# ScalarE takes the rows' mean and variance, VectorE a PSUM copy: a fused embed, attention and FFN kernel

## The reference

```python
h = concatenate([patch_rows, text_rows], axis=1)          # 64 x 228 x 192
h = h + attention(layernorm(h))
h = h + ffn(layernorm(h))

def bitlinear(x, w, g):
    xn = rmsnorm(x, g)                    # x * rsqrt(mean(x*x) + 1e-6) * g
    xq = act_quant(xn)                    # per row: round(xn * 127 / max|xn|), and back
    return einsum('bsd,fd->bsf', xq, ternary(w))
def ffn(x):
    return bitlinear(gelu(bitlinear(x, w1, g1)), w2, g2)   # 192 -> 768 -> 192
```

## Time and profile before

| what | value |
|---|---|
| median of 3 runs | 1753.07 us (1752.8 to 1753.71) |
| the profiled execution | 1751.31 us |
| its span, first to last instruction | 1749.6 us |
| mean granted TensorE clock | 0.913 |
| PE busy | 1473.4 us (84%) |
| DVE busy | 1461.2 us (84%) |
| ACT busy | 1232.4 us (70%) |
| POOL busy | 1099.7 us (63%) |

### The profile page before, as it was taken

How to read it: one execution, slowest core, us unless ns; L and a number is a source line. 1 busy time by engine, 2 the same in 40 slices (tenths; PEclk the granted TensorE clock), 3 DMA queues, 4 the chain that set the end, 5 groups by cost and what they waited for, 6 DMA issues and landing times.

```text
span 1749.6 us, 53766 instructions
## 1 busy us (share of the span) xinstructions
PE 1473.4 (84%) x18602; PEld 1203.6 (69%) x18602; DVE 1461.2 (84%) x3227; ACT 1232.4 (70%) x1862; POOL 1099.7 (63%) x1369
## 2 busy tenths in 40 slices
PE   5799999999999999999999999985556565656565
PEld 2688888888888888888888888874454454544454
DVE  5588888888888888888888888874899999999996
ACT  0476666667676776767667676653688888888887
POOL 5456565656666665666665656542777777777775
PEclk9899999999999999999999999996677877777876
DMA  8533334343434343434343333320000000000000
GB/s 209 78 60 68 61 63 65 61 67 60 68 60 68 59 69 55 72 53 74 53 72 56 70 58 68 60 56 18 9 24 20 24 20 24 20 24 20 24 20 29
DMA packets 104194, 93.57 MB, mean 53 GB/s; under 512 B 22737, under 2 KB 94466, under 8 KB 104162
## 3 DMA queue, kind: packets, MB, share of 16 engines
q1 hardware_dynamic: 103394, 91.58, 27.7%
q0 software_dynamic: 768, 1.57, 0.4%
HBM read 74.12 MB, written 11.91 MB: 49 GB/s over the span
## 4 chain that ended last, share of the span: by engine, by line
PE 66%; DVE 20%; issue 7%; ACT 3%; POOL 1%; DVEq 1%; DMA 0%; SPq 0%; ACTq 0%; POOLq 0%
PE ps L1039 19%; PE ps L1096 9%; PE ps L1182 8%; DVE nmax L677 6%; PE ps L1173 5%; PE ps L1129 5%; DVE ff_st L813 4%; PE ps L1280 3%; PE ps L1161 3%; PE ps L1155 3%; PE ps L1261 3%; PE ps L1134 2%; PE ps L1077 2%; PE ps L1110 2%; DVE xpix L806 1%
## 5 line engine op out<-in xcount | busy, mean ns | idle before, releaser
L1039 PE MATMUL ps<-w_eff,pix 124*112 124x193 f32 (+1 forms) x2048 | 406.8, 337 | 10.4 <-DMA pix<-side 8.4
L677 DVE TENSOR_REDUCE nmax<-ps 116x12 bf16<-116x1344 f32 (+2 forms) x192 | 302.9, 1577 | 87.1 <-PE ps L1134 87.1
L493 POOL TENSOR_TENSOR pix<-probs,g_b 112x192 f32<-112x192 f32 (+1 forms) x512 | 298.0, 612 | 103.5 <-ACT probs L994 94.2
L882 ACT ACTIVATE probs<-ps,isw 116x688 f32<-116x688 f32 x384 | 298.9, 831 | 84.6 <-PE ps L1161 83.2
L1039 PEld LDWEIGHTS ps<-w_eff,pix 124*112 124x112 f32 (+1 forms) x2048 | 308.3, 167 | 37.2 <-issue 22.0
L420 POOL TENSOR_TENSOR xsq<-xsq 124x784 f32<-124x784 f32 (+1 forms) x128 | 184.4, 1441 | 216.1 <-ACT xsq L875 211.1
L440 POOL TENSOR_SCALAR_AFFINE_SELECT probs<-probs 116x464 f32<-116x464 f32 x384 | 274.1, 726 | 68.9 <-ACT probs L882 60.4
L1250 PE MATMUL ps<-ident_h,xpix 112*96 112x112 f16 (+1 forms) x256 | 34.9, 281 | 193.8 <-DVE xpix L830 187.9
L864 ACT ACTIVATE pix<-xpix 54x896 f32<-54x896 f32 (+1 forms) x128 | 196.6, 1538 | 1.2 <-DMA xpix<-in_x 0.4
L1096 PE MATMUL ps<-xnT,wq_pad 97*128 97x228 f32 (+1 forms) x768 | 166.5, 366 | 0.0
L1250 PEld LDWEIGHTS ps<-ident_h,xpix 112*96 112x96 f16 (+1 forms) x256 | 23.8, 167 | 205.0 <-issue 103.3
(11 more groups left out here) (134 smaller groups left out, 3175.1 us busy)
## 6 DMA issues: line engine op xcount, KB each, us to landing
xpix<-in_x SPq DMA_DIRECT2D x192, 196.0 KB
rden<-den_rows SPq DMA_DIRECT2D x256, 85.5 KB, 2.2
out<-xpix SPq DMA_DIRECT2D x64, 87.0 KB
out<-xpix SPq DMA_DIRECT2D x64, 84.0 KB
xpix<-in_x SPq DMA_DIRECT2D x128, 34.1 KB
h_all<-shift_w SPq DMA_DIRECT2D x5, 768.0 KB, 4.4
pix<-side SPq DMA_DIRECT2D x64, 36.8 KB
pix<-side SPq DMA_DIRECT2D x64, 36.6 KB
```

Source lines behind the costliest of these rows:

```text
L493: last = nc.gpsimd.tensor_tensor(v2[0:P, b, tile, cols], gel[0:P, b, tile, cols], g2_b[0:P, cols], ALU.mult)
L677: V.tensor_reduce(dst, src, AX_X, ALU.max, negate=True).then_inc(s_mx, 1)
L882: A(probs[0:TB, g, 2 * e:2 * e + 2, :], ps[0:TB, 4 + 2 * e:6 + 2 * e, 0:SK], ACT.Exp, scale=isw[0:TB, 7:8]).then_inc(s_p, 1)
L1039: last = MM(ps_tok[tile][0:P, :], pix[0:HI, par, o, lo:lo + P], w_eff[0:HI, o, :], start=(o == 0), stop=(o == OFFS - 1))
```

## The change

The mean and the variance of the FFN's input rows move from VectorE in the FFN stage to ScalarE in the attention stage. `row_means(n - 1)` sums a row with a Copy of scale -1/192 into `mean2`, `row_squares(n - 1)` sums (h - mean)^2 into `row_ssq`, each with the accumulator of the ACTIVATE, two tiles each. GpSimd's `row_roots(n - 2)` turns that into the roots and keeps them for all images in `roots`. In the FFN stage VectorE no longer runs bn_stats, bn_aggr and the first mean square; it copies the turned rows (`copy_rows_turned`, which ScalarE did), and the product scales are a separate instruction (`weigh_steps`, with a semaphore `f_step`). Its order is now v1, y, copy_rows_turned, weigh_steps, max of v1, mean square of gelu, max of v2, the chain, q1. ScalarE's order is quantise, squares, copy of q2T, gelu; the squares of image i are now in step i. TensorE's order is turn_first(m), turn_second(j), ffn_first(m), ffn_second(j). GpSimd's pow in the FFN stage has two columns.

```diff
+            def row_roots(m):
+                pool.wait_ge(s_rsq, 2 * m + 2)
+                after(pool, s_rms, m)
+                apart(pool)
+                nc.gpsimd.tensor_scalar(ln_st[:, 32:34], row_ssq[:, :], (1.0 + EPS_RMS) / DIM, EPS_LN * EPS_RMS,
+                                        ALU.mult, ALU.add).then_inc(s_var2, 1)
+                pool.wait_ge(s_var2, m + 1)
+                nc.gpsimd.tensor_tensor(roots[:, bass.ds(m * 4, 2)], ln_st[:, 32:34], expo[:, 0:2],
+                                        ALU.pow).then_inc(s_rms, 1)
...
                 if newer:
                     patch_roots(n + 2)
+                if prev:
+                    row_roots(n - 2)
                 if old:
                     clear_later(n, 0)
...
+            def copy_rows_turned(m):
+                dve.wait_ge(f_t1, m + 1)
+                after(dve, f_m1, 2 * m)
+                src = bank16(0, 4 * TB, F16).rearrange("p (t c k) -> p t c k", t=2, c=2)
+                for tile, P in enumerate((TA, TB)):
+                    ins = V.tensor_scalar(q1T[0:HALF, tile, :, 0:P], src[0:HALF, tile, :, 0:P], -MAGIC16, None, ALU.add)
+                ins.then_inc(f_t1s, 1)
+
+            def weigh_steps(i, b):
+                after(dve, f_g, 2 * i)
+                V.tensor_tensor(ff_st[:, b, 40:44], ff_st[:, b, 28:32], w_step[:, :], ALU.mult).then_inc(f_step, 1)
...
-                if new:
-                    apart(dve)
-                    for tile, P in enumerate((TA, TB)):
-                        ins = V.bn_stats(st[0:P, 6 * tile:6 * tile + 6], h_all[0:P, hcols(m, tile)])
-                    flink(ins)
-                    apart(dve)
-                    for tile, P in enumerate((TA, TB)):
-                        ins = V.bn_aggr(st[0:P, 12 + 2 * tile:14 + 2 * tile], st[0:P, 6 * tile:6 * tile + 6])
-                    flink(ins)
...
+                if turned:
+                    copy_rows_turned(m - 1)
+                if steps_:
+                    weigh_steps(i - 1, 1 - b)
...
                 if mid:
-                    dve.wait_ge(f_v2, 2 * j + 2)
+                    dve.wait_ge(f_ssq, 2 * j + 2)
+                    V.tensor_scalar(st[:, 18:20], gel_sum[:, 1 - b, :], 1.0 / HIDDEN, EPS_RMS, ALU.mult,
+                                    ALU.add).then_inc(f_var, 1)
...
-                    V.tensor_tensor(st[:, 40:44], st[:, 28:32], w_step[:, :], ALU.mult)
...
+            def row_means(n):
+                act.wait_ge(s_h2, n + 1)
+                after(act, s_rsq, 2 * n)
+                apart(act)
+                for tile, P in enumerate((TA, TB)):
+                    A(spare[0:P, tile, :], h_all[0:P, hcols(n, tile)], ACT.Copy, scale=-1.0 / DIM,
+                      accum_out=mean2[0:P, bass.ds(n * 2 + tile, 1)]).then_inc(s_mean2, 1)
+
+            def row_squares(n):
+                after(act, s_var2, n)
+                for tile, P in enumerate((TA, TB)):
+                    act.wait_ge(s_mean2, 2 * n + tile + 1)
+                    apart(act)
+                    A(spare[0:P, tile, :], h_all[0:P, hcols(n, tile)], ACT.Square,
+                      bias=mean2[0:P, bass.ds(n * 2 + tile, 1)],
+                      accum_out=row_ssq[0:P, tile:tile + 1]).then_inc(s_rsq, 1)
...
                 if newest:
                     edge_squares(n + 3, par)
+                if prev:
+                    row_means(n - 1)
                 if old:
                     copy_attended(n, 2, 3)
...
                     regroup_even(n + 4, 1 - par, coming, 0)
+                if prev:
+                    row_squares(n - 1)
                 if new:
                     copy_maxima(n + 1)
...
-            def ffn_step(i, new=True, mid=True, last_=True):
+            def ffn_step(i, new=True, mid=True):
                 if new:
                     turn_first(i + 1)
-                if last_:
-                    ffn_second(i - 2)
+                if mid:
+                    turn_second(i - 1)
                 if new:
                     ffn_first(i + 1)
                 if mid:
-                    turn_second(i - 1)
+                    ffn_second(i - 1)
```

More of the change, by code:

```diff
@@ L527, in _ @@
             step(V.memset(ff_st[:, :, :], 1.0))
+            step(V.memset(mean2[:, :], 1.0))
+            step(V.memset(row_ssq[:, :], 1.0))
+            step(V.memset(roots[:, :], 1.0))
             step(V.memset(gel_sum[:, :, :], 1.0))
@@ L727, in step_images @@
                     maxima(n + 1, 0)
+                if new:
                     maxima(n + 1, 1)
@@ L768, in ffn_step @@
+            def weigh_steps(i, b):
+                after(dve, f_g, 2 * i)
+                V.tensor_tensor(ff_st[:, b, 40:44], ff_st[:, b, 28:32], w_step[:, :], ALU.mult).then_inc(f_step, 1)
+            def ffn_step(i, b, new=True, mid=True, last_=True, turned=True, steps_=True, skipped=0):
                 m, j, st = i + 1, i - 1, ff_st[:, b, :]
                 flinks[:] = [0, (i + 1) * F_LINKS - skipped]
-                if new or mid:
-                    after(dve, f_g, 2 * i)
-                    after(dve, f_q2, i - 2)
@@ L834, in _ @@
             dve.wait_ge(s_h2, IMAGES - 1)
-            ffn_step(-1, 1, mid=False, last_=False)
+            dve.wait_ge(s_rms, 1)
+            dve.wait_ge(s_mean2, 2)
+            ffn_step(-1, 1, mid=False, last_=False, turned=False, steps_=False)
+            copy_rows_turned(0)
+            weigh_steps(-1, 1)
             step_images(IMAGES, 1, None, old=False, new=False, newer=False)
             dve.wait_ge(s_h2, IMAGES)
-            ffn_step(0, 0, mid=False, last_=False)
+            dve.wait_ge(s_rms, IMAGES)
+            dve.wait_ge(s_mean2, 2 * IMAGES)
+            ffn_step(0, 0, mid=False, last_=False, turned=False, steps_=False)
             ffn_step(1, 1, last_=False)
@@ L947, in _ @@
             act.wait_ge(s_vset, V_SETUP)
-            step_images(-2, 1, 1, 2, old=False, new=False)
-            step_images(-1, 0, 0, 2, old=False)
+            step_images(-2, 1, 1, 2, prev=False, old=False, new=False)
+            step_images(-1, 0, 0, 2, prev=False, old=False)
             act.wait_ge(s_text[1], 64)
-            step_images(0, 1, 1, 3)
+            step_images(0, 1, 1, 3, prev=False)
             step_images(1, 0, 0, 3)
@@ L976, in quantise, with ffn_step @@
                     ins.then_inc(f_q2, 1)
-            def ffn_step(i, b, new=True, mid=True):
+            def ffn_step(i, b, new=True, mid=True, squares=True):
                 m, j = i + 1, i - 1
-                if new:
-                    act.wait_ge(f_t1, m + 1)
-                    after(act, f_m1, 2 * m)
-                    for tile, P in enumerate((TA, TB)):
-                        src = bank16(0, 4 * TB, F16).rearrange("p (t c k) -> p t c k", t=2, c=2)
-                        ins = A(q1T[0:HALF, tile, :, 0:P], src[0:HALF, tile, :, 0:P], ACT.Copy, bias=-MAGIC16)
-                    ins.then_inc(f_t1s, 1)
                 if mid:
@@ L989, in ffn_step @@
                     quantise(i, b, 1)
-                if new:
-                    after(act, f_v2, 2 * m - 2)
+                if squares:
+                    after(act, f_var, i - 1)
                     for tile, P in enumerate((TA, TB)):
-                        act.wait_ge(f_m1, 2 * m + tile + 1)
-                        A(gel[0:P, 1 - b, tile, :].rearrange("p (c d) -> p c d", c=2),
-                          ps[0:P, 2 + 2 * tile:4 + 2 * tile, 0:HIDDEN // 2], ACT.Gelu,
-                          scale=ff_st[0:P, b, 40 + tile:41 + tile]).then_inc(f_g, 1)
+                        act.wait_ge(f_g, 2 * i + tile + 1)
+                        A(gsq[0:P, tile, :], gel[0:P, b, tile, :], ACT.Square,
+                          accum_out=gel_sum[0:P, b, tile:tile + 1]).then_inc(f_ssq, 1)
                 if mid:
@@ L1004, in ffn_step @@
                 if new:
-                    after(act, f_var, m - 1)
+                    after(act, f_v2, 2 * m - 2)
+                    act.wait_ge(f_step, m + 1)
                     for tile, P in enumerate((TA, TB)):
-                        act.wait_ge(f_g, 2 * m + tile + 1)
-                        A(gsq[0:P, tile, :], gel[0:P, 1 - b, tile, :], ACT.Square,
-                          accum_out=gel_sum[0:P, 1 - b, tile:tile + 1]).then_inc(f_ssq, 1)
-            ffn_step(-1, 1, mid=False)
-            act.wait_ge(s_h2, IMAGES)
+                        act.wait_ge(f_m1, 2 * m + tile + 1)
+                        A(gel[0:P, 1 - b, tile, :].rearrange("p (c d) -> p c d", c=2),
+                          ps[0:P, 2 + 2 * tile:4 + 2 * tile, 0:HIDDEN // 2], ACT.Gelu,
+                          scale=ff_st[0:P, b, 40 + tile:41 + tile]).then_inc(f_g, 1)
+            ffn_step(-1, 1, mid=False, squares=False)
+            row_means(IMAGES - 1)
+            row_squares(IMAGES - 1)
             ffn_step(0, 0, mid=False)
@@ L1021, in _ @@
             ffn_step(IMAGES - 1, 1, new=False)
-            ffn_step(IMAGES, 0, new=False)
```

(1 more changed line is left out.)

96 lines of the change are left out of this document (53 added, 43 removed).

## The result

The changed kernel takes 1691.39 us (median of 4 runs, 1690.73 to 1693.28) beside 1752.93 us for the kernel before (median of 4, 1751.3 to 1753.71): a ratio of 0.965, 95% interval 0.9635 to 0.9669. It is 61.5 us faster. The profiled execution took 1690.73 us, its span is 1689.0 us.

What follows compares the result with a forecast made beforehand. VectorE was taken to set the FFN stage's pace, TensorE the attention stage's, where the change costs nothing. VectorE's step falls from 7.93 to 7.51 us, 25.6 us over 61 steps, less 1.2 once: 1728 us, range 1696 to 1752.

Steps and rivals of the forecast that it cites:

- VectorE's step: FFN stage: the time of VectorE's instructions for one step, said to set the pace; 7.51 us new, 7.93 old.
- v1 beside the products: VectorE's FFN step: v1's pair runs within GpSimd's products and costs 0.65 us plus 0.40 for the stretch.
- the copies: VectorE's FFN step: the two added f16 copies of turned rows from PSUM cost 0.70 us, bounds 0.55 and 0.90.
- weigh_steps: VectorE's FFN step: this added instruction of 4 elements costs 0.35 us, between 0.15 and 0.50.
- mean square: VectorE's FFN step: the mean square of gelu comes when GpSimd's products are over and costs about 0.12 us.
- (b): FFN stage: loop from scales through quantise, ScalarE's squares, mean square, maxima and chain; 6.86 us, 0.65 shorter than VectorE's step.
- rival A: FFN stage: v1 unstretched, copies 0.55, so the squares' loop sets the pace; step 6.9 to 7.1, 1697 us; chance 0.20.
- the likeliest case: FFN stage: VectorE's step is 7.25 to 7.75 us; 1728 us in all, own range 1713 to 1743; chance 0.50.
- The attention stage at nothing: Attention stage: the work added on ScalarE (0.8 to 1.0 us a pair) and GpSimd (1.05) is hidden, costing nothing.
- rival C: Attention stage: GpSimd's row_roots, from 1.45 us, delays clear_later(1) and TensorE waits; 1774 us at 2.2; chance 0.12.
- Once each: Costs outside the repeated steps: +1.2 us before the second FFN step; the tail keeps its chain.

Runs made afterwards that it cites:

- experiment 4: Changed kernel with ScalarE's squares moved back behind its copy of q2T (quantise, copy, squares, gelu): 1867.72 us, ratio 1.0657.
- experiment 6: Changed kernel with GpSimd multiplying only the first quarter of each row of gelu by g2: 1675.62 us, ratio 0.9563.
- experiment 7: Changed kernel with y ahead of v1 in VectorE's order (y, v1, copies): 1691.72 us, ratio 0.965.
- experiment 5: Changed kernel with VectorE's copies done a second time, into an f32 buffer nobody reads: 1722.8 us, ratio 0.982.
- experiment 2: Experiment 1 plus the FFN stage using the kept means and roots; ScalarE still copies the turned rows, all orders as before: 1747.37 us, ratio 0.9965.
- experiment 9: Changed kernel with bn_stats, bn_aggr and the first mean square put back on VectorE ahead of v1, results unread: 1759.02 us, ratio 1.0034.
- experiment 1: Kernel before plus row_means, row_squares and row_roots in the attention stage, results unused, FFN stage unchanged: 1749.25 us, ratio 0.9984.
- experiment 3: Changed kernel, but ScalarE copies the turned rows, between its squares and the copy of q2T: 1711.06 us, ratio 0.9754.
- experiment 8: Changed kernel with y ahead of v1 and the mean square between the two maxima of v2: 1689.79 us, ratio 0.9639.
- experiment 10: Changed kernel with TensorE's order of before (turn_first, ffn_second of image i - 2, ffn_first, turn_second): 1817.36 us, ratio 1.0368.

## Why the prediction was wrong

The step of the prediction that failed is its sum for VectorE's step, 7.51 us, and with it the claim that VectorE sets the pace. Three terms of the sum were too large: v1 beside the products, the copies and weigh_steps. VectorE's own step came out at 6.92. That is below the loop through the squares, which was forecast at 6.86 and measured 7.04, and the longer of the two is the step. Forecast and measured terms of VectorE's step, start to start, the latter as a mean over 43 steps (1300 to 1612 us) of the changed kernel (the last column is measured less forecast; the terms are rounded):

| term | forecast | measured | difference |
|---|---|---|---|
| chain of small operations to q1 | 1.32 | 1.36 | +0.04 |
| q1 to v1 | 0.87 | 1.04 | +0.17 |
| v1 | 1.05 | 0.72 | -0.33 |
| y | 0.65 | 0.65 | 0 |
| copies | 0.70 | 0.37 | -0.33 |
| weigh_steps | 0.35 | 0.07 | -0.28 |
| maximum of v1, with the wait for the squares | 0.53 | 0.64 | +0.11 |
| mean square | 0.12 | 0.22 | +0.10 |
| maxima of v2 | 1.92 | 1.98 | +0.06 |
| sum | 7.51 | 7.04 | -0.47 |

0.47 x 63 is 30 of the 37 us between forecast and result.

**The squares' loop**, in the terms of the forecast's (b): from the scales to quantise 0.37 (forecast 0.21), quantise 1.67 (1.65), squares 1.75 (1.76), on to the mean square 0.03 (0.06), mean square 0.22 (0.12), maxima of v2 1.98 (1.92), chain 1.03 (1.14). That is 7.04, the whole step, beside 6.86. So what came is rival A, with its mechanism and its step of 6.9 to 7.1, and the likeliest case fell. A's two conditions hold, v1 nearly unstretched and copies at their least, but the copies lie 0.18 below that least. Experiments 4, 6 and 7 agree with the loop as the pace, and experiment 5 shows how near beneath it VectorE's own step lies.

**Below the range.** The step isn't what put the result below 1696. With the measured 7.04 the forecast's own sum, (7.93 - 7.04) x 61 less 1.2, gives 1700 us. The other 9 are 63 steps in place of 61 (1.8 us), the 1.2 that was never spent, the stage's earlier start (2.7), the shorter tail (1.7) and about 1 by which the medians differ from the profiled executions. The range's lower end was A's middle and had no room for these.

**The copies.** I bounded them from below by the nearest rows with f32 elements, 0.53 and 0.65 a pair, and wrote 0.55. A copy of f16 elements from PSUM into f16 takes 258 ns at its median and 0.37 a pair. Experiment 5 has the same source into f32, at 0.60, so the size of the elements written decides. The Trainium skill (VectorE: DVE Perf Modes, Why PSUM operands drop a tier) says that an operand in PSUM leaves a 16-bit instruction a mode of twice the rate and an f32 one none; the two measured pairs agree. All rows of the trace of before that I took bounds from were f32, so nothing in them bounded an f16 copy from below.

**v1 beside the products.** The place was right (L811 at 1510.57 lies within GpSimd's products, 1508.31 to 1513.46). The one row of 756 ns did stand beside a product (v1 at 1234.68, the product at 1234.63 and 0.59 us long), but to take it as the price was wrong. Experiment 6 measures the stretch here at 0.04 a pair. Yet there is a stretch at other alignments: 1.15 a pair in the steps shown of experiments 2 and 9, 0.93 in the mean in experiment 7. The Trainium skill's rule (GPSIMD Engine Reference, Key points: GpSimd contends with VectorE instructions that have two SBUF inputs) agrees as to v1 taking part; that section doesn't say who loses. Here it is GpSimd. Its products of the changed kernel, grouped by shape, 1400 to 1600 us:

```profile
L517 POOL TENSOR_TENSOR pix<-probs,g_b 116x192 f32<-116x192 f32 x114 | 74.7, 683 | 4.0
L517 POOL TENSOR_TENSOR pix<-probs,g_b 112x192 f32<-112x192 f32 x113 | 67.0, 622 | 21.4 <-ACT probs L1057 21.4
```

The same pieces took 632 and 591 ns before, so all eight pieces together are 0.33 us longer, as against 4.85 in the earlier trace rows, 5.15 now. GpSimd had room for it.

**weigh_steps** starts behind the copies and costs its issue, 0.07, not 0.35. **What I missed the other way:** v1 waits for q1's end (0.17 more, the idle 0.20 ahead of L811), a wait that the new order adds and that I did not price. The mean square waits 0.12 for the squares, which shows in the distance behind the maximum of v1. And I had it behind the products' end; at 1513.06 it still stands beside them (they end at 1513.46) and takes 0.43 in place of 0.17, as in every second step.

**What bounded the kernel before** was told only half. "VectorE sets the pace" is right as a reading of its rows, and experiment 2 shows that the other half was missing: relieving VectorE alone is worth 0.3%, of which the attention part has 0.2. The working did put the squares' loop of the new order beside VectorE's step, but never that of the old order. The forecast did not depend on it, for the change moves the orders too; an engineer who had made only the first half of the change would have been misled by it.

**The attention stage at nothing** held as to cost (experiment 1), with two of its terms in other sizes and a gain of 0.07 us an image, 4 us in all, that I had not seen. ScalarE in order of time:

```profile
603.15 0.36 ACT L952 ACTIVATE spare<-h_all 112x192 f32 x1
603.40 0.20 ACT L952 ACTIVATION_READ_ACCUMULATOR spare<-h_all  x1
...
604.45 0.36 ACT L929 ACTIVATE o_sb<-ps 128x228 f32<-128x228 f32 x1 [0.51 <-PE ps L1224]
```

row_means takes 0.80 of the hole of 1.24 from 603.15 to the read-out's end and leaves 0.51. The estimate from the Trainium skill in the prediction, 346 ns, agrees with the median of 362 measured (L952), and its 439 for the squares with 444 (L960). GpSimd:

```profile
614.30 0.62 POOL L446 TENSOR_SCALAR ln_st<-row_ssq 128x2 f32<-128x2 f32 x1
615.11 0.95 POOL L449 TENSOR_TENSOR roots<-ln_st,expo 128x2 f32 x1 [0.19 <-POOL ln_st L446]
616.02 2.26 POOL L459 TENSOR_SCALAR_AFFINE_SELECT probs<-probs 116x464 f32<-116x464 f32 x4
```

row_roots takes 1.76 and not 1.05, beyond the 1.45 at which rival C was to begin, and TensorE still doesn't wait: clear_later for both groups is done by 618.28, as the four pieces take 2.26 in place of 3.13 (1.81 and 1.32) before. I had taken their price as fixed. What the pieces stood beside has changed. Before, and then in the changed kernel:

```profile
614.07 1.81 POOL L440 TENSOR_SCALAR_AFFINE_SELECT probs<-probs 116x464 f32<-116x464 f32 x2
614.65 1.44 DVE L638 SCALAR_TENSOR_TENSOR h_all<-tok_t,front_st,bw 112x192 f32 x2
```

```profile
614.77 0.74 DVE L664 SCALAR_TENSOR_TENSOR h_all<-tok_t,front_st,bw 112x192 f32 x2
```

L638 took 751 ns in the mean in the 124 cases with a clear beside it, and 413 in the 4 without. row_roots now stands at that place, the clears come behind it, and both get shorter: between 300 and 1000 us the same instruction (L664) has a median of 407 ns in place of 746, and a clear a mean of 599 in place of 727. Experiment 1 has the same (407 and 603) with the FFN stage of before, so it is the attention part that does this. It accounts for the 11 us that VectorE is less busy in 300. How the 0.07 an image follows from it, through TensorE, was not traced.

**Once each:** I had 1.2 us more at the start of the stage; it starts 2.7 earlier, and the tail is 1.7 shorter. The shorter tail is in all runs with the new orders (13.4 to 14.2 us, 15.4 in the kernel before and in experiment 1). The start can't be read that finely: in the profiles of the changed kernel and of experiments 2 to 10, which have the same attention code, the last addition to `h_all` starts at 1221.1 to 1227.7 us, and at 1227.6 before.

**The parts need each other.** The attention part alone gives 4 us, the statistics off VectorE as well 6, the new orders with ScalarE's copy 42, the copy on VectorE 61; with the statistics still on VectorE the new orders and the copy give -6. The change shortens two loops that stood level, and each hides the gain of the other while it is left as it was.

## What to carry to other kernels

An engine without idle time may still not be the only bound: before relieving it, sum the longest loop that passes through it and its neighbours, in the old order as well as in the new one. A wait can hide where no idle bracket stands: an instruction that starts at the same few ns behind its releaser in every step is held by it. Bound a cost from below only by rows with the same element size and the same memory: the size of the elements written alone took a pair of PSUM copies from 0.60 to 0.37 us. When two loops are level, an edit that relieves one of them shows nothing by itself, and that is no verdict on the edit.

## What the runs showed of the hardware

- GpSimd can pay beside VectorE instructions with two tensors from SBUF. In the changed kernel its tensor_scalar of two elements (L446) takes 191 to 193 ns in the 4 cases with no such instruction beside it and 561 to 622 in the 60 beside VectorE's L713 and L664; its pow of two elements (L449) takes 688 to 690 in the same 4 and 912 in the mean in the 60 beside L664 and L690. L664 itself keeps its 402 to 413 ns there, and takes 670 to 766 in the 4 cases beside a clear. So who of the two pays differs from one pair of instructions to the next.
- VectorE's v1 pair has been 0.75, 0.79, 0.93 and 1.15 us long, for the same instructions on the same data. The last two stood at least in part beside GpSimd's products, and so did the 0.79.
- VectorE's instructions of two to four elements take 0.15 to 0.6 us, the same instruction in one kernel too: L839 161 to 519 ns, experiment 5's L805 0.06 to 0.51 from start to start. The long ones are those beside GpSimd: in the changed kernel L839 takes 168 to 171 ns in the 30 FFN steps in which GpSimd is idle and 360 to 519 in the 31 beside its products, and L805 142 to 148 without GpSimd and 310 to 579 with it (1240 to 1670 us).
- TensorE's granted clock in the FFN window fell from 0.78 to 0.74 although TensorE was busy 150 of 200 us and not 122. Both are means over stretches at 2.4 GHz and at 1.2. Little of it can have reached the time: in these 200 us ScalarE waited for TensorE's results for 5.7 us, and VectorE never.
